# Graph attention block on one core: contexts before scores in every step

## Chip, cores and metric

One core of a Trainium2 chip. The metric is the device time of one execution in microseconds (us), here the median of three. One execution was also taken by the hardware profiler; the rows below are from it.

## What is computed

The input x is 128 graphs of 128 nodes with 384 features, adj is a 128x128 mask for each graph. All is float32.

```python
q = heads(x @ Wq + bq); k = heads(x @ Wk + bk); v = heads(x @ Wv + bv)   # 6 heads of 64
scores = einsum('bhqd,bhkd->bhqk', q, k) / sqrt(64)
probs = softmax(scores + where(adj, 0, -9e15)[:, None], axis=-1)
ctx = einsum('bhqk,bhkd->bhqd', probs, v)
y = x + (merge(ctx) @ Wf + bf)
out = (y - mean(y)) / sqrt(var(y) + 1e-5)      # over the 384 features
```

## The kernel before, in words

The work goes by **pairs** of graphs, 64 in all; a graph of a pair is called e=0 or e=1. Each engine has its own hand-written order of work, and semaphores alone join them. A **step** handles several stages of different pairs at once. In step p TensorE makes, in this order (`step`, L487):

- the scores of pair p (`scores`, L384; matmuls on L395): 6 heads for each graph, with 64 rows of the array each;
- the contexts of pair p-2 (`ctx_product`, L399; L413): 6 heads for each graph, with 64 columns of the array each;
- two of the three q/k products that this step has for a group of four graphs ahead (`qk_product`, L418), 9 matmuls of 512 columns each;
- the output products of pair p-2 (`out_product`, L429), 9 matmuls of 384 columns each;
- the third q/k product;
- the v products of pair p+2 (`early_v`, L444), again 9 of 384 columns each.

The q/k, output and v products are sums of three: high times high, low times high and high times low part (`split_product`, L375, matmuls on L379 to L381). So each operand has a high part, rounded by ScalarE, and a low part, which VectorE forms as the difference.

The banks of PSUM: `scores_ps` has two for each graph of the pair, `qk_ps` two, `cov_ps` one for each e. Three products share `cov_ps[e]` in turn: the contexts, the output product, and the v product. So before the contexts are made, `ctx_product` waits for `v_copied` of the previous step's v product, which ScalarE copies out (`copy_v`, L795); and before the v product is made, `early_v` waits for `y_added`, VectorE's addition of the output product and x (`add_residual`, L627; L638). `ctx_product` also waits for `pT_landed`: the probabilities are turned in blocks of 32x32 by VectorE, stored to DRAM and loaded again in transposed block order, all by DMAs of the SP queue (`store_blocks`, L288, and `load_blocks`, L295). `scores` waits for q and k (`qk_copied`) and until the scores of the pair before have been read (`max_found`).

VectorE in step p (`step`, L662): `mask_and_max` for both graphs (L606: adds the mask, scales, takes row maxima; L612 negates them), `split_ctx` (low parts of the contexts of pair p-2, L580), `turn_x` (transposes x of pair p+4, L588), `invert_sums` for e=0 (L625), `turn_blocks` for e=0 (L618), `invert_sums` for e=1, `split_x` for both (low parts of x^T of pair p+4, L595), `add_residual` for both (L638), then statistics of e=0, `turn_blocks` for e=1, and statistics of e=1.

ScalarE in step p (`step`, L810): `round_ctx` for both graphs (L781, high parts of the contexts), `exps` of e=0 (six on L790), a q/k copy (L807), `exps` of e=1, a q/k copy, `round_x` for both (high parts of x^T, L775), the third q/k copy, and the two copies of v (L798).

GpSimd in step p (`step`, L924): `make_mask_bias` for the two graphs of pair p+1 (L896; each waits until VectorE has read the mask of the same e, `max_found`), `add_bias` for both (L903), `normalise_probs` for both (L920, each waits for VectorE's inverted sums), `normalise_y` for pair p-2 (L909, L915).

`run_steps` (L82) writes the first steps out, runs a loop of four steps a turn, and writes the last out; step 61 is the last one of it. Pairs 62 and 63 are finished by `ending` (L527), which has its own order. Contexts begin in step 2, and v products on `cov_ps` end with step 59; x^T is also made ahead up to step 59.

Of the kernel before, what the change touches and what calls it, by code (L numbers as in the profile page):

```python
# [35 lines left out]
PAIRS = BATCH // 2  # L36
# [9 lines left out]
LAG = 2  # L46
# [22 lines left out]
def real(n, count):  # L69

    return not isinstance(n, int) or 0 <= n < count


def past(eng, sem, n, per=1):

    value = (n + 1) * per
    if isinstance(value, int) and value <= 0:
        return
    eng.wait_ge(sem, value)
# [14 lines left out]
def attention_block(nc, x, adj, wq, bq, wk, bk, wv, bv, wf, bf, out):  # L94
    ctx = ExitStack()
    with ctx:
# [81 lines left out]
        def ctx_bank(e, n):  # L178

            return qk_ps[e] if isinstance(n, int) and n >= 2 * (ENDING + 1) else cov_ps[e]  # L180
# [5 lines left out]
        def by_matmul(n):  # L186

            return isinstance(n, int) and n < BY_MATMUL
# [185 lines left out]
        def _(pe):  # L374
# [9 lines left out]
            def scores(i, c, e, n):  # L384
                par = c // 2 % 2
                if e == 0:
                    past(pe, qk_copied, 2 * i + c // 2, per=NJ)
                    if isinstance(n, int) and n == 0:
                        pe.wait_ge(xT_split, BY_MATMUL)
                        pe.wait_ge(bias_row_ready, 1)  # L390
                past(pe, max_found, n - 2)
                tok = tokens(2 * c + e)
                for h in range(HEADS):
                    rows = slice(h % 2 * HEAD, (h % 2 + 1) * HEAD)
                    last = nc.tensor.matmul(scores_ps[:, score_cols(e, h)], qT[rows, par, h // 2, tok],  # L395
                                            kT[rows, par, h // 2, tok], start=True, stop=True)
                last.then_inc(scores_done, 1)

            def ctx_product(i, c, p, e):  # L399
                n, at = 2 * (p - LAG) + e, 2 * (c - LAG) + e  # L400
                if isinstance(n, int) and n >= BY_VECTOR:
                    pe.wait_ge(pT_copied, 2 * (n - BY_VECTOR + 1))
                else:
                    past(pe, pT_landed[at % PT_RING], 2 * i + at // PT_RING, per=BLOCKS * DMA)
                if isinstance(p, int) and p - 1 + AHEAD >= ENDING:
                    past(pe, y_added, n - 2 if n < 2 * (ENDING + 1) else n - 4)
                    past(pe, v_copied, n)
                else:
                    past(pe, v_copied, 2 * (p - 1 + AHEAD) + e)
                dst = ctx_bank(e, n)  # L410
                for h in range(HEADS):
                    half = h % 2 * HEAD
                    last = nc.tensor.matmul(dst[half:half + HEAD, h // 2 * SEQ:(h // 2 + 1) * SEQ],  # L413
                                            v_sb[:, at % V_RING, h * HEAD:(h + 1) * HEAD],
                                            pT[:, at % PT_RING, :, h, :], start=True, stop=True)
                last.then_inc(ctx_done, 1)

            def qk_product(i, c, j):  # L418
                mat, m = QK_JOBS[j]
                g, par = 2 * i + (c + AHEAD) // 2, (c + AHEAD) // 2 % 2  # L420
                if isinstance(g, int) and g == 0:
                    pe.wait_ge(w_split[mat], m + 1)
                past(pe, xT_split, g * GROUP + GROUP - 1)
                past(pe, qk_copied, g * NJ + j - 2)
                split_product(qk_ps[j % 2][:, :], lambda k: (
                    w_hi[mat][:, k, m * P:(m + 1) * P], w_lo[mat][:, k, m * P:(m + 1) * P],
                    xT_hi[:, par, k, :], xT_lo[:, par, k, :]), qk_done)

            def out_product(c, p, e):  # L429
                n = 2 * (p - LAG) + e  # L430
                if isinstance(p, int) and p == LAG:
                    pe.wait_ge(w_split["f"], KC)
                pe.wait_ge(cT_split, n + 1)
                if isinstance(n, int) and n >= 2 * (ENDING + 1):
                    past(pe, y_added, n - 2)
                split_product(cov_ps[e][:, 0:HID], lambda k: (
                    cT_hi[:, e, k, :], cT_lo[:, e, k, :], w_hi["f"][:, k, :], w_lo["f"][:, k, :]), out_done)
# [6 lines left out]
            def early_v(c, p, e):  # L444
                n = 2 * (p + AHEAD) + e
                if isinstance(n, int) and n == 0:
                    pe.wait_ge(w_split["v"], KC)
                past(pe, xT_split, n)
                if real(p - LAG, PAIRS):
                    past(pe, y_added, 2 * (p - LAG) + e)  # L450
                else:
                    past(pe, v_copied, n - 2)
                v_product(cov_ps[e], 2 * (c + AHEAD) + e)
# [9 lines left out]
            def transpose_x(n):  # L463
                past(pe, x_loaded[n % X_RING], 0, per=DMA)
                past(pe, xT_split, n - 4)
                for k in range(KC):
                    last = nc.tensor.transpose(xT_bank(n)[:, k * SEQ:(k + 1) * SEQ],  # L467
                                               x_in[:, n % X_RING, k * P:(k + 1) * P], ident[:, :])
                last.then_inc(xT_done, 1)

            def warm_up(n):


                for _ in range(n):
                    nc.tensor.transpose(qk_ps[1][:, 0:P], ident[:, :], ident[:, :])  # L475

            def bias_product():

                pe.wait_ge(w_loaded["f"], DMA)
                pe.wait_ge(bv_widened, 1)  # L480
                pe.wait_ge(xT_split, GROUP + 1)
                for k in range(KC):
                    last = nc.tensor.matmul(xT_bank(0)[:, 0:HID], bv_wide[:, k, :], w_raw["f"][:, k, :],  # L483
                                            start=k == 0, stop=k == KC - 1)
                last.then_inc(bias_mm, 1)

            def step(i, c):  # L487
                p = TURN * i + c
                jobs = list(range(c % 2 * HALF, (c % 2 + 1) * HALF)) if real(p + AHEAD, PAIRS) else []
                if real(p, PAIRS):  # L490
                    for e in range(2):
                        scores(i, c, e, 2 * p + e)
                if real(p - LAG, PAIRS):
                    for e in range(2):
                        ctx_product(i, c, p, e)
                for j in jobs[:2]:
                    qk_product(i, c, j)
                if isinstance(p, int) and by_matmul(2 * (p + X_AHEAD)):
                    for e in range(2):
                        n = 2 * (p + X_AHEAD) + e  # L500
                        transpose_x(n)
                        if n in WARM_UPS:
                            warm_up(WARM_UPS[n])
                if isinstance(p, int) and p == -1:
                    bias_product()
                if real(p - LAG, PAIRS):
                    for e in range(2):
                        out_product(c, p, e)
                for j in jobs[2:]:
                    qk_product(i, c, j)  # L510
                if real(p + AHEAD, ENDING):
                    for e in range(2):
                        early_v(c, p, e)
# [50 lines left out]
            pe.wait_ge(ident_ready, 2)  # L564
            warm_up(WARM_UPS[-1])
            run_steps(pe, step, ENDING)
            ending()

# [414 lines left out]
```

## Time and profile before

| what | value |
|---|---|
| median of three runs | 1030.92 us (1030.38 to 1031.15) |
| the profiled execution | 1031.09 us |
| its span, first to last instruction | 1029.3 us |
| mean granted clock of TensorE | 0.999 |
| TensorE busy | 1017.5 us, 99% |
| weight loads | 906.5 us, 88% |
| VectorE busy | 732.1 us, 71% |
| GpSimd busy | 627.8 us, 61% |
| ScalarE busy | 596.4 us, 58% |

How to read it: an engine's busy time is the union of its instructions. TensorE's matmuls are pipelined, so that their durations overlap, and the distance from one start to the next is what counts. PE is TensorE, PEld its weight loads, DVE VectorE, ACT ScalarE, POOL GpSimd, and SPq the queue of the sync engine, which issues nearly all DMAs. One row of a timeline may stand for several instructions alike (x2, x24); its duration is then from the first's start to the last's end.

### The profile page before, as it was taken

How to read it: one execution, taken by the hardware profiler on the slowest of the kernel's cores; microseconds unless marked ns; L12 is line 12 of the kernel's file. 1: busy time of each engine (PE TensorE's matmuls, PEld its weight loads, DVE VectorE, ACT ScalarE, POOL GpSimd, SP SyncE). 2: the span in 40 equal slices, each digit the busy share in tenths (PEclk: the TensorE clock that was granted, in tenths of full speed). 3: DMA queues.
4: the chain of work that ended last, by engine and by line, in shares of the span. 5: the costliest groups of instructions: out<-in, count | busy, mean ns of one | idle time of the engine just before them, and what ended most of it. 6: DMA issues, size and time to landing. Idle time of an engine off the chain costs nothing.

```text
span 1029.3 us, 26790 instructions
## 1 busy us (share of the span) xinstructions
PE 1017.5 (99%) x7185; PEld 906.5 (88%) x7185; DVE 732.1 (71%) x2822; ACT 596.4 (58%) x2127; POOL 627.8 (61%) x649
## 2 busy tenths in 40 slices
PE   8999999999999999999999999999999999999996
PEld 7889889889888898898888898888988988988886
DVE  3576777777677777767776776777777677767674
ACT  4565655656646656556556466465565565564563
POOL 1355666656665756656666566656566666666675
PEclk9999999999999999999999999999999999999999
DMA  7286676676666666766766766766667667666431
GB/s 197 77 209 183 174 192 159 177 193 164 181 183 168 189 177 171 195 166 173 193 161 175 192 162 185 186 166 190 172 172 196 165 176 184 166 176 183 146 122 62
DMA packets 337690, 176.48 MB, mean 171 GB/s; under 512 B 222336, under 2 KB 321792, under 8 KB 337664
## 3 DMA queue, kind: packets, MB, share of 16 engines
q1 hardware_dynamic: 336864, 175.79, 62.7%
q10 hardware_dynamic: 800, 0.39, 0.1%
q8 instruction: 11, 0.18, 0.1%
q14 instruction: 15, 0.12, 0.0%
HBM read 102.18 MB, written 73.92 MB: 171 GB/s over the span
## 4 chain that ended last, share of the span: by engine, by line
PE 98%; DVE 1%; issue 0%; ACT 0%; POOL 0%; POOLq 0%; DVEq 0%
PE qk_ps L379 14%; PE qk_ps L381 13%; PE qk_ps L380 13%; PE cov_ps L379 13%; PE cov_ps L381 13%; PE cov_ps L380 13%; PE scores_ps L395 9%; PE cov_ps L413 9%; PE qk_ps L475 0%; PE scores_ps L523 0%; DVE s_mask L606 0%; DVE xT_lo L595 0%; PE scores_ps L467 0%; PE scores_ps L483 0%; PE qk_ps L413 0%
## 5 line engine op out<-in xcount | busy, mean ns | idle before, releaser
L790 ACT ACTIVATE probs<-s_mask,neg_max 128x128 f32<-128x128 f32 x756 | 292.6, 390 | 4.3 <-DVE neg_max L612 4.3
L606 DVE CUSTOM_DVE_ANT_0 s_mask<-scores_ps,mask_bias 128x128 f32<-128x128 f32 x768 | 172.5, 287 | 89.8 <-PE scores_ps L395 85.9
L920 POOL TENSOR_TENSOR probs<-probs,inv_sum 128x768 f32<-128x768 f32 x126 | 186.0, 1477 | 78.2 <-DVE inv_sum L625 78.2
L915 POOL TENSOR_SCALAR y_sb<-y_sb,mean_var,rstd 128x384 f32<-128x384 f32 x124 | 205.2, 1655 | 22.8 <-POOL rstd L909 22.8
L618 DVE STREAM_TRANSPOSE p_turned<-probs 128x768 f32<-128x768 f32 x124 | 121.3, 978 | 113.3 <-POOL probs L920 113.3
L909 POOL TENSOR_TENSOR rstd<-var_eps,minus_half 128x1 f32<-128x1 f32 x128 | 72.5, 566 | 180.3 <-DVE var_eps L653 180.3
L807 ACT ACTIVATE qT<-qk_ps,bq_col 128x512 f32<-128x512 f32 x96 | 65.6, 683 | 155.4 <-PE qk_ps L381 155.4
L790 ACT ACTIVATION_READ_ACCUMULATOR probs<-s_mask,neg_max 128x1 f32 x756 | 142.7, 189 | 0.0
L595 DVE TENSOR_TENSOR xT_lo<-xT,xT_hi 128x384 fp32r<-128x384 f32 x120 | 113.2, 981 | 32.8 <-ACT xT_hi L775 32.6
L781 ACT CAST cT_hi<-cov_ps 128x384 fp32r<-128x384 f32 x126 | 60.5, 480 | 125.8 <-PE cov_ps L413 123.0
L798 ACT COPY v_sb<-cov_ps 128x384 f32<-128x384 f32 x124 | 59.5, 480 | 122.0 <-PE cov_ps L381 122.0
L379 PE MATMUL cov_ps<-wf_hi,cT_hi 128*128 128x384 f32 x384 | 129.3, 337 | 0.0
L381 PE MATMUL cov_ps<-wf_hi,cT_lo 128*128 128x384 f32 x384 | 129.1, 336 | 0.0
L380 PE MATMUL cov_ps<-wf_lo,cT_hi 128*128 128x384 f32 x384 | 128.7, 335 | 0.0
L903 POOL TENSOR_TENSOR x_bias<-x_in,bias_row 128x384 f32<-128x384 f32 x128 | 127.6, 1019 | 0.0
L379 PE MATMUL cov_ps<-wv_hi,xT_hi 128*128 128x384 f32 x372 | 124.8, 336 | 0.9 <-DVE wv_lo L574 0.9
L381 PE MATMUL cov_ps<-wv_hi,xT_lo 128*128 128x384 f32 x372 | 124.9, 336 | 0.0
L380 PE MATMUL cov_ps<-wv_lo,xT_hi 128*128 128x384 f32 x372 | 124.7, 335 | 0.0
L379 PE MATMUL qk_ps<-xT_hi,wq_hi 128*128 128x512 f32 x288 | 116.0, 403 | 0.2 <-DVE xT_lo L595 0.2
L379 PE MATMUL qk_ps<-xT_hi,wk_hi 128*128 128x512 f32 x288 | 115.4, 401 | 0.0
L381 PE MATMUL qk_ps<-xT_hi,wq_lo 128*128 128x512 f32 x288 | 113.8, 395 | 0.0
L380 PE MATMUL qk_ps<-xT_lo,wq_hi 128*128 128x512 f32 x288 | 113.5, 394 | 0.0
(76 smaller groups left out, 2007.4 us busy)
## 6 DMA issues: line engine op xcount, KB each, us to landing
p_out<-p_turned SPq DMA_DIRECT2D x124, 384.0 KB, 2.6
pT<-p_out SPq DMA_DIRECT2D x496, 96.0 KB, 2.4
x_in<-in_x SPq DMA_DIRECT2D x128, 192.0 KB, 3.5
out<-y_sb SPq DMA_DIRECT2D x128, 192.0 KB, 2.4
x_blocks<-in_x SPq DMA_DIRECT2D x360, 64.0 KB, 2.3
adj_u<-in_adj SPq DMA_DIRECT2D x32, 64.0 KB, 3.3
probs<-in_L_gnn_Wv SPq DMA_DIRECT2D x1, 576.0 KB, 6.2
pT<-in_L_gnn_Wf SPq DMA_DIRECT2D x1, 576.0 KB, 6.8
```

Source lines behind the costliest of these rows:

```text
L379: nc.tensor.matmul(dst, s_hi, m_hi, start=k == 0, stop=False)
L380: nc.tensor.matmul(dst, s_hi, m_lo, start=False, stop=False)
L381: last = nc.tensor.matmul(dst, s_lo, m_hi, start=False, stop=k == n_chunks - 1)
L395: last = nc.tensor.matmul(scores_ps[:, score_cols(e, h)], qT[rows, par, h // 2, tok], kT[rows, par, h // 2, tok], start=True, stop=True)
L413: last = nc.tensor.matmul(dst[half:half + HEAD, h // 2 * SEQ:(h // 2 + 1) * SEQ], v_sb[:, at % V_RING, h * HEAD:(h + 1) * HEAD], pT[:, at ...
L595: nc.vector.tensor_tensor(xT_lo[:, par, :, tok], xT_source(n, e), xT_hi[:, par, :, tok].bitcast(F32), ALU.subtract).then_inc(xT_split, 1)
L606: last = nc.vector.tensor_tensor_reduce(out=s_mask[:, e, h, :], in0=scores_ps[:, score_cols(e, h)], in1=mask_bias[:, e, :], scale=SCALE, s ...
L618: nc.vector.transpose(p_turned[:, e, :, :, :].rearrange("p b h j -> p h b j"), probs[:, e, :, :].rearrange("p h (b k) -> p h b k", b=BLOCK ...
L790: last = nc.scalar.activation(p_sb[:, e, h, :], s_mask[:, e, h, :], ACT.Exp, bias=neg_max[:, e, h:h + 1], scale=1.0, accum_out=row_sum[:, ...
L903: nc.gpsimd.tensor_tensor(x_bias[:, slot, :], x_in[:, slot, :], bias_row[:, :], ALU.add).then_inc(x_biased, 1)
L915: nc.gpsimd.tensor_scalar(y_sb[:, y, :], y_sb[:, y, :], mean_var[:, e, 0:1], rstd[:, e, 0:1], ALU.subtract, ALU.mult).then_inc(y_ready, 1)
L920: nc.gpsimd.tensor_tensor(p_sb[:, e, :, :], p_sb[:, e, :, :], inv_sum[:, e, :].unsqueeze(2).broadcast_to([P, HEADS, SEQ]), ALU.mult).then_ ...
```

## The change

In TensorE's step the contexts of pair p-2 come first and the scores of pair p second. Nothing else is altered, neither the waits inside the two functions nor the order of any other engine, nor `ending`.

```diff
             def step(i, c):
                 p = TURN * i + c
                 jobs = list(range(c % 2 * HALF, (c % 2 + 1) * HALF)) if real(p + AHEAD, PAIRS) else []
+                if real(p - LAG, PAIRS):
+                    for e in range(2):
+                        ctx_product(i, c, p, e)
                 if real(p, PAIRS):
                     for e in range(2):
                         scores(i, c, e, 2 * p + e)
-                if real(p - LAG, PAIRS):
-                    for e in range(2):
-                        ctx_product(i, c, p, e)
                 for j in jobs[:2]:
                     qk_product(i, c, j)
```

## Rows read from the trace of the kernel before

**Rows 1.** The page, busy time of each engine (us, share of the span, instructions).

```profile
PE 1017.5 (99%) x7185; PEld 906.5 (88%) x7185; DVE 732.1 (71%) x2822; ACT 596.4 (58%) x2127; POOL 627.8 (61%) x649
```

**Rows 2.** Timeline of TensorE, step 30 (start us, us, engine, line, operation, tiles).

```profile
493.32 1.61 PE L395 MATMUL scores_ps<-kT,qT 64*128 64x128 f32 x24
494.86 1.53 PE L413 MATMUL cov_ps<-pT,v_sb 128*64 128x128 f32 x24
496.32 0.50 PE L379 MATMUL qk_ps<-xT_hi,wq_hi 128*128 128x512 f32 x1
...
500.53 0.33 PE L379 MATMUL cov_ps<-wf_hi,cT_hi 128*128 128x384 f32 x1
...
508.98 1.61 PE L395 MATMUL scores_ps<-kT,qT 64*128 64x128 f32 x24
```

**Rows 3.** Timeline of VectorE, step 30.

```profile
497.47 0.09 DVE L606 DVE_READ_ACCUMULATOR2_ANT row_max<- 128x1 f32 x1
...
497.67 1.01 DVE L580 TENSOR_TENSOR cT_lo<-cov_ps,cT_hi 128x384 fp32r<-128x384 f32 x2
...
501.52 0.98 DVE L618 STREAM_TRANSPOSE p_turned<-probs 128x768 f32<-128x768 f32 x1 [1.83 <-POOL probs L920]
...
503.13 1.88 DVE L595 TENSOR_TENSOR xT_lo<-xT,xT_hi 128x384 fp32r<-128x384 f32 x2 [0.55 <-ACT xT_hi L775]
504.93 1.01 DVE L638 TENSOR_TENSOR y_sb<-cov_ps,x_bias 128x384 f32<-128x384 f32 x2
```

**Rows 4.** Timeline of GpSimd, step 30.

```profile
497.70 0.30 POOL L896 TENSOR_SCALAR mask_bias<-adj_u 128x128 f32<-128x128 uint8 x1 [1.30 <-issue]
497.97 2.00 POOL L903 TENSOR_TENSOR x_bias<-x_in,bias_row 128x384 f32<-128x384 f32 x2
499.91 1.48 POOL L920 TENSOR_TENSOR probs<-probs,inv_sum 128x768 f32<-128x768 f32 x1
502.65 1.47 POOL L920 TENSOR_TENSOR probs<-probs,inv_sum 128x768 f32<-128x768 f32 x1 [1.26 <-DVE inv_sum L625]
```

**Rows 5.** Timeline of ScalarE and of TensorE's weight loads, step 30.

```profile
496.43 0.48 ACT L781 CAST cT_hi<-cov_ps 128x384 fp32r<-128x384 f32 x1 [0.17 <-PE cov_ps L413]
496.81 0.40 ACT L790 ACTIVATE probs<-s_mask,neg_max 128x128 f32<-128x128 f32 x1
...
505.59 0.19 PEld L379 LDWEIGHTS cov_ps<-wv_hi,xT_hi 128*128 128x128 f32 x1
...
509.08 0.48 ACT L798 COPY v_sb<-cov_ps 128x384 f32<-128x384 f32 x1 [1.08 <-PE cov_ps L381]
```

**Rows 6.** Timeline of step 1, which has no contexts.

```profile
43.20 1.61 PE L395 MATMUL scores_ps<-kT,qT 64*128 64x128 f32 x24
...
45.92 0.40 ACT L790 ACTIVATE probs<-s_mask,neg_max 128x128 f32<-128x128 f32 x1 [2.14 <-DVE neg_max L612]
...
52.24 2.30 DVE L595 TENSOR_TENSOR xT_lo<-xT,xT_hi 128x384 fp32r<-128x384 f32 x2
...
52.28 1.85 POOL L920 TENSOR_TENSOR probs<-probs,inv_sum 128x768 f32<-128x768 f32 x1 [1.16 <-DVE inv_sum L625]
...
54.47 0.96 DVE L618 STREAM_TRANSPOSE p_turned<-probs 128x768 f32<-128x768 f32 x1
```

**Rows 7.** Timeline of the end of step 7 and the start of step 8.

```profile
144.04 0.55 DVE L595 TENSOR_TENSOR xT_lo<-xT,xT_hi 128x384 fp32r<-128x384 f32 x1
...
144.51 1.01 DVE L638 TENSOR_TENSOR y_sb<-cov_ps,x_bias 128x384 f32<-128x384 f32 x2
...
148.50 0.38 PE L395 MATMUL scores_ps<-kT,qT 64*128 64x128 f32 x2
```

**Rows 8.** Busy time of each engine in two stretches, granted clock, DMA.

```profile
15.00:20.00 5.00, 4.11 (x23) 3.65 (x22) 4.21 (x8) 2.40 (x5) 2.61 (x5) 1.00 0.80 143
1020.00:1029.00 9.00, 2.09 (x13) 1.77 (x11) 5.45 (x16) 0.00 (x0) 1.98 (x3) 0.88 0.24 88
```

## The prediction

> **What bounds the kernel now.** I first read the page's busy times, to see which engine sets the time: TensorE is busy 99% of the span, the next engine 71% [rows 1]. Next TensorE's timeline over one step, to see the order and whether there are holes: the scores of pair 30 start at 493.32, the contexts of pair 28 at 494.86, the q/k products at 496.32, the output products at 500.53, the next scores at 508.98 [rows 2]. A step is 15.66 us without a hole. The scores block holds 1.54 us, the contexts block 1.46.
>
> That only says that TensorE is never late now. What counts is how late its inputs may come, so I then read VectorE, GpSimd and ScalarE in the same step. Write S for the start of the scores. The last maximum is read at 497.47 (S+4.15). GpSimd's second mask waits for it (497.70), then come the two x+bias (497.97, 2.00 us for both) and the first normalisation of the probabilities (499.91, 1.48) with no gap [rows 3, 4]. VectorE waits for that, turns the blocks (501.52) and inverts the second sums; this releases GpSimd's second normalisation (502.65 to 504.12). The low parts of x^T start at 503.13 and the two take 1.88, where one without GpSimd beside it takes 0.55 [rows 7]: the first is not finished until GpSimd is. The residual additions start at 504.93. Two take 1.01 overlapping by 0.08 (503.13+1.88 against 504.93), so one takes 0.545 and the first ends at 505.47, **S+12.15** [rows 3, 4]. The v product that follows overwrites the bank which this addition reads, and its first weight load is at 505.59, 0.12 later [rows 5]. TensorE starts no weight load more than one matmul ahead, so a hole would open if this one came much later. So a chain of 12.15 us, which starts with the scores and runs through the other engines, is only just in time for the v product; I put its slack at 0 to 0.1 us.
>
> **The change, part by part.** It adds and removes nothing: per step 24 context and 24 score matmul records trade places; no DMA and no queue but TensorE's is touched. Call C the start of the step.
>
> 1. *TensorE's own time*: the same three changes of shape (v to first block, first to second, second to q/k). In today's order the blocks hold 1.54 and 1.46, 3.00 together [rows 2]; I take 3.00 again, 0. Bounds: plus or minus 0.05 a step.
>
> 2. *The wait of the second context for its bank.* The contexts write the banks that ScalarE copies v out of. The copy of the second v runs 509.08 to 509.56, 0.58 after the step's start [rows 5]; today 1.54 us of scores cover it. With the 0.12 us from a finish to the weight load behind it, the second context could load at C+0.70, and its matmuls follow when half the block, 0.73, has passed; now the load can't run ahead of them. Between 0 and 0.15 us; I take 0.08, the middle.
>
> 3. *The scores and all that hangs on them start later*: at C+1.46+0.08 = C+1.54. That is the cost that matters, since the chain of 12.15 us hangs on S, and the v product's place in TensorE's order hangs on C. Unchanged, the addition would end at C+13.69 where it now ends at S+12.15.
>
> 4. *What gets shorter in the chain.* ScalarE's first exponentials now start at 496.81 (S+3.49), behind the high part of the second context (496.43, 0.48) [rows 5]. In pair 1, which has no contexts yet, they start at 45.92, S+2.72, as soon as the maxima are there [rows 6]. After the change the contexts come first, so ScalarE follows pair 1, and the high parts of x^T, which follow the exponentials on it, come 0.77 earlier. But that alone doesn't shorten the chain, since GpSimd's part (mask, x+bias, normalisation) hangs on the maxima and not on ScalarE. Pair 1 shows what then happens: VectorE starts the first low part at 52.24, S+9.04, just before GpSimd starts its normalisation at 52.28. The first low part is through at once, the normalisation takes 1.85 instead of 1.47, the second low part waits for it, and the pair ends at 54.54, S+11.34 [rows 4, 6]. An addition of 0.545 that begins at 54.47 (where pair 1 has its next work) ends at 55.015, **S+11.81**. Pair 1 has no low parts of contexts on VectorE; I add 0.03 for them and take **S+11.84**.
>
> The Trainium skill ("SBUF — State Buffer", section "Who interferes with whom") says of this that a VectorE instruction with two SBUF inputs and a GpSimd instruction that reads SBUF exclude each other, and that the first to issue keeps the ports for its whole length. The 1.85 us of rows 6 agree. By the rule alone the order of 52.24 and 52.28 decides the case, as in the first rival below.
>
> 5. *From the addition to the next step.* Where the addition already came a little late, it began at 144.51 (first one over at 145.055) and the next step began at 148.50: 3.45 us [rows 7]. Late release costs nothing beyond this; VectorE, ScalarE and GpSimd have their later work behind TensorE's v products as now.
>
> Sum of a step: 1.54 + 11.84 + 3.45 = 16.83 us, against 15.66: **+1.17 us**, all of it TensorE standing before the v product. It hits the steps that have contexts, low parts of x^T and a v product: pairs 2 to 59, 58 steps, 67.9 us. In pairs 60 and 61 no v product waits; the end sees the scores of pair 61 later by between 0 and 1.5 us, of which I take half, 0.7. Together 68.6. The profiled execution took 1031.09 (span 1029.30), 0.17 over the median of 1030.92: 1030.92 + 68.6 = **1099.5 us**.
>
> *What stays covered.* The output products need the low parts of the contexts: the first pair of these starts at 497.67, and one takes 0.54, so S+4.89; that becomes C+6.43 and TensorE wants them at C+7.21 [rows 2, 3]. The probabilities' way through DRAM: VectorE has the first half of pair 30 turned at 502.50, the second some 6 us later, and the contexts read them two steps on, at 494.86+31.3 = 526.2; 17 us for a store and a load, of which 3.1 go (scores 1.54 later, contexts 1.54 earlier). If these covers were gone, each us would count 58 times.
>
> **The rivals.**
> - *GpSimd's normalisation comes first.* The 0.04 us in pair 1 is a knife's edge. If GpSimd wins, both low parts wait for it: today's order, with the normalisation at pair 1's S+9.08 plus the same 0.03 in place of today's S+9.33 [rows 4, 6], so the addition ends 0.22 before S+12.15, at S+11.93: +1.26 a step, 73.1+0.7, **1104.7 us**.
> - *Nothing in the chain gets shorter*: S+12.15 stays: 1.54+12.15+3.45 = 17.14, +1.48 a step, 85.8+0.7, **1117.4 us**. For it: the steady steps all show S+12.15. Against it: pair 1, and that GpSimd's last y ends earlier against S once the step is longer.
> - *Not slower*: both low parts pass ahead of the normalisation. Then they run from S+9.04 to about S+10.1, the addition ends at S+10.6 = C+12.1, and the v product is in time. It decides at C+12.2: below this, no stall. With the copy of v also early enough (item 2 at 0) the time is **1031 us**, with 0.08 a step 1035.6. Against it: in pair 1 the second low part stood directly behind the first on VectorE and yet lost to GpSimd [rows 6].
> - *The clock*: the granted clock is 1.00 in a stretch with TensorE busy 4.11 of 5 us and 0.88 in the last 9 us, where it is busy 2.09 [rows 8]. A hole of 1.2 us in 16.8 is nearer to the first. If one step in ten ran at 1.2 instead of 2.4 GHz, it would take some 15 us longer: 1099.5+5.8x15, **1186 us**. The Trainium skill ("TensorE: Matmul & The Clock Gate", Part 1) has the clock halve after idleness; both rows agree with that, and neither shows it for holes this short.
> - The change does what it says: no other place sets the order of the two blocks on TensorE, and the steps of the loop all pass through it.
>
> **How the numbers follow.** Forecast 0.45, GpSimd first 0.25, nothing shorter 0.12, not slower 0.05, clock 0.03; 0.10 for a stall that is shorter or longer through something I don't see. The likeliest gives 1099.5. Downwards item 2 at 0 takes 4.6 off, item 1 2.9, the end 0.7, and the unseen shorter chains reach somewhat further: 1086. Upwards "nothing shorter" sets 1118. Not slower splits into 0.03 within 0.2% (some 2 us, about what a measurement of this kernel can tell from no change) and 0.01 below; its rest is slower.
>
> **What would show it.** Right: a step of 16.8 us; a hole of about 1.2 us on TensorE before the first weight load of the v product, released by VectorE's residual addition; exponentials at S+2.7; the first low part of x^T short and the normalisation beside it 1.85. If both low parts are in one long pair and the normalisation 1.47, it is the first rival. Wrong: the hole stands elsewhere (before the second context, or before the output products), or the step stays near 15.7.

## The result, and the profile after

The changed kernel took a median of 1104.73 us (1104.40 to 1105.13) against 1030.67 for the kernel before on the same chip: a ratio of 1.0717, 95% interval 1.0700 to 1.0734. It is 74.1 us slower, or 1.28 us for each of the 58 steps that the forecast counts. The forecast was 1099.5 us (1086 to 1118), slower with 0.96.

The page of the profile after: span, busy times, TensorE's granted clock in 40 slices, and the chain that ended last.

```profile
span 1102.6 us, 26790 instructions
...
PE 1036.0 (94%) x7185; PEld 901.9 (82%) x7185; DVE 749.0 (68%) x2822; ACT 602.3 (55%) x2127; POOL 644.2 (58%) x649
...
PEclk9999999999999999999999999999999999999999
...
PE 40%; issue 26%; POOL 18%; DVE 13%; DVEq 1%; ACT 1%; POOLq 0%; ACTq 0%
```

The instructions are as many as before. TensorE's share falls from 99% [rows 1] to 94%, and no other engine rises. The chain has moved off TensorE: GpSimd and VectorE now hold a third of it.

TensorE's waits after, by what ended them (us in total, times, longest):

```profile
PE cov_ps L379 <- DVE y_sb L638: 55.0, 58, 1.0
```

One wait, 58 times: the first matmul of the v product for VectorE's residual addition. These 55.0 us are counted from modelled ends of matmuls, and the hole costs more than that. By starts, in the step below, the v product begins 1.36 us after the last q/k matmul (557.57 to 558.93), and in step 30 before 0.23:

```profile
505.53 0.40 PE L381 MATMUL qk_ps<-xT_hi,wq_lo 128*128 128x512 f32 x1
505.76 0.34 PE L379 MATMUL cov_ps<-wv_hi,xT_hi 128*128 128x384 f32 x1
```

Its second matmul follows 0.25 later instead of 0.18. That makes 1.20 us a step, some 70 us; the rest of the 1.28 is in the contexts' block, as shown further down.

Step 31 after, TensorE (start us, us; C is 545.29 and S is 546.83):

```profile
545.29 1.61 PE L413 MATMUL cov_ps<-pT,v_sb 128*64 128x128 f32 x24
546.83 1.61 PE L395 MATMUL scores_ps<-kT,qT 64*128 64x128 f32 x24
...
552.58 0.33 PE L379 MATMUL cov_ps<-wf_hi,cT_hi 128*128 128x384 f32 x1
...
557.57 0.40 PE L381 MATMUL qk_ps<-xT_hi,wq_lo 128*128 128x512 f32 x1
558.93 0.41 PE L379 MATMUL cov_ps<-wv_hi,xT_hi 128*128 128x384 f32 x1 [0.96 <-DVE y_sb L638]
...
562.22 1.53 PE L413 MATMUL cov_ps<-pT,v_sb 128*64 128x128 f32 x24
```

The same step on VectorE, on ScalarE, and on GpSimd:

```profile
550.98 0.08 DVE L606 DVE_READ_ACCUMULATOR2_ANT row_max<- 128x1 f32 x1
...
555.93 0.15 DVE L625 RECIPROCAL inv_sum<-row_sum 128x6 f32<-128x6 f32 x1
556.01 2.30 DVE L595 TENSOR_TENSOR xT_lo<-xT,xT_hi 128x384 fp32r<-128x384 f32 x2
558.24 1.01 DVE L638 TENSOR_TENSOR y_sb<-cov_ps,x_bias 128x384 f32<-128x384 f32 x2
```

```profile
545.40 0.48 ACT L798 COPY v_sb<-cov_ps 128x384 f32<-128x384 f32 x1 [1.08 <-PE cov_ps L381]
...
549.69 0.40 ACT L790 ACTIVATE probs<-s_mask,neg_max 128x128 f32<-128x128 f32 x1 [2.28 <-DVE neg_max L612]
```

```profile
551.21 0.30 POOL L896 TENSOR_SCALAR mask_bias<-adj_u 128x128 f32<-128x128 uint8 x1 [1.38 <-issue]
...
556.15 1.74 POOL L920 TENSOR_TENSOR probs<-probs,inv_sum 128x768 f32<-128x768 f32 x1 [1.26 <-DVE inv_sum L625]
```

Read against [rows 2 to 5]: C to S is 1.54 in this step. The last maximum is read at S+4.15, as before. The exponentials start at S+2.86 instead of S+3.49 and now wait for the maxima instead of the contexts' high parts. GpSimd's second mask is at S+4.38, where it was. The low parts of x^T start at S+9.18, before GpSimd's second normalisation at S+9.32. That normalisation takes 1.74 instead of 1.47, the pair of low parts 2.30 instead of 1.88, and it is over at S+11.48, where it was over at S+11.69. The first addition ends at 558.24+0.545 = 558.785, which is S+11.95, and the next step begins 3.44 later. 1.54 + 11.95 + 3.44 = 16.93 us, where a step took 15.66.

The four steps of a loop turn are not alike. Steps 32 and 33:

```profile
562.22 1.53 PE L413 MATMUL cov_ps<-pT,v_sb 128*64 128x128 f32 x24
563.68 1.61 PE L395 MATMUL scores_ps<-kT,qT 64*128 64x128 f32 x24
...
579.07 1.68 PE L413 MATMUL cov_ps<-pT,v_sb 128*64 128x128 f32 x24
580.68 1.61 PE L395 MATMUL scores_ps<-kT,qT 64*128 64x128 f32 x24
```

C to S is 1.46 in the first step of a turn, 1.61 in the second and third and 1.54 in the fourth, the same in every turn; the mean of the 58 steps is 1.55. In the old order the contexts' block holds 1.46 in each step. S to the first addition is 11.94 to 11.97 in nearly all steps of the loop. The whole step has a mean of 16.95 us against 15.67.

### The profile page after: what moved, and what is told of

The parts are those of the page before. It is cut to its first block, busy times and chain, and to the rows that moved or that the text cites. A ratio compares the mean times of both kernels' runs of the same rounds, so it can differ in the third digit from the quotient of the medians.

```text
span 1102.6 us, 26790 instructions
## 1 busy us (share of the span) xinstructions
PE 1036.0 (94%) x7185; PEld 901.9 (82%) x7185; DVE 749.0 (68%) x2822; ACT 602.3 (55%) x2127; POOL 644.2 (58%) x649
## 4 chain that ended last, share of the span: by engine, by line
PE 40%; issue 26%; POOL 18%; DVE 13%; DVEq 1%; ACT 1%; POOLq 0%; ACTq 0%
POOL x_bias L903 9%; PE cov_ps L413 9%; DVE s_mask L606 8%; PE cov_ps L379 8%; POOL probs L920 8%; PE cov_ps L381 6%; PE cov_ps L380 6%; PE scores_ps L395 5%; DVE y_sb L638 3%; PE qk_ps L379 1%; PE qk_ps L380 1%; PE qk_ps L381 1%; DVEq L79 1%; DVE xT_lo L595 1%; DVE inv_sum L625 1%
## 5 line engine op out<-in xcount | busy, mean ns | idle before, releaser
L920 POOL TENSOR_TENSOR probs<-probs,inv_sum 128x768 f32<-128x768 f32 x126 | 201.5, 1600 | 78.1 <-DVE inv_sum L625 78.1
L379 PE MATMUL cov_ps<-wv_hi,xT_hi 128*128 128x384 f32 x372 | 128.9, 347 | 55.9 <-DVE y_sb L638 55.0
L896 POOL TENSOR_SCALAR mask_bias<-adj_u 128x128 f32<-128x128 uint8 x128 | 38.1, 298 | 188.4 <-DVE row_max L606 103.3
L595 DVE TENSOR_TENSOR xT_lo<-xT,xT_hi 128x384 fp32r<-128x384 f32 x120 | 138.2, 1192 | 0.2
L379 PEld LDWEIGHTS cov_ps<-wv_hi,xT_hi 128*128 128x128 f32 x372 | 69.7, 187 | 80.2 <-DVE xT_lo L595 78.7
```

The source lines that it names most:

```text
L379: nc.tensor.matmul(dst, s_hi, m_hi, start=k == 0, stop=False)
L595: nc.vector.tensor_tensor(xT_lo[:, par, :, tok], xT_source(n, e), xT_hi[:, par, :, tok].bitcast(F32), ALU.subtract).then_inc(xT_split, 1)
L920: nc.gpsimd.tensor_tensor(p_sb[:, e, :, :], p_sb[:, e, :, :], inv_sum[:, e, :].unsqueeze(2).broadcast_to([P, HEADS, SEQ]), ALU.mult).then_ ...
```

## The experiments

Each time below stands beside one of the kernel before, whose median was 1030.8 to 1031.2 us in these sets. The first four experiments ask whether the chain from the scores to the addition carries the cost.

**1. Additions ahead of the low parts, contexts first.** On VectorE, in the changed kernel:

```diff
                     invert_sums(1, 2 * p + 1)
+                if real(p - LAG, PAIRS):
+                    for e in range(2):
+                        add_residual(i, c, e, 2 * (p - LAG) + e)
                 if real(p + X_AHEAD, PAIRS):
                     for e in range(2):
                         split_x(c, e, 2 * (p + X_AHEAD) + e)
...
                 if real(p - LAG, PAIRS):
-                    for e in range(2):
-                        add_residual(i, c, e, 2 * (p - LAG) + e)
                     find_stats(c, 0, 2 * (p - LAG))
```

> The changed order, and on VectorE the two residual additions moved ahead of the two low parts of x^T. Theory: the change costs time only because the additions stand at the end of a chain that starts with the scores, and the v product waits for them. The additions then end by about S+10.3 (S: start of the scores), which is C+11.8 (C: start of the step), ahead of the v product's place at C+12.2; the hole of 1 us goes, the step is 15.67 us plus 0 to 0.1 for the second context's wait for the copy of v, and the time is 1031 to 1037 us. Rival: the order itself costs TensorE time (changes of shape, the contexts' wait): then nothing comes back, about 1104 us.

Measured: 1037.06 us (1036.42 to 1037.13), ratio 1.0055 (1.0038 to 1.0071). Of the 74.1 us, 68.2 are gone. VectorE and TensorE in a step of it (S is 513.69):

```profile
522.78 0.15 DVE L625 RECIPROCAL inv_sum<-row_sum 128x6 f32<-128x6 f32 x1
522.85 0.98 DVE L638 TENSOR_TENSOR y_sb<-cov_ps,x_bias 128x384 f32<-128x384 f32 x2
523.75 1.62 DVE L595 TENSOR_TENSOR xT_lo<-xT,xT_hi 128x384 fp32r<-128x384 f32 x2
```

```profile
512.15 1.61 PE L413 MATMUL cov_ps<-pT,v_sb 128*64 128x128 f32 x24
513.69 1.61 PE L395 MATMUL scores_ps<-kT,qT 64*128 64x128 f32 x24
...
522.41 0.33 PE L381 MATMUL cov_ps<-wf_hi,cT_lo 128*128 128x384 f32 x1
...
524.66 0.33 PE L379 MATMUL cov_ps<-wv_hi,xT_hi 128*128 128x384 f32 x1
...
527.90 1.53 PE L413 MATMUL cov_ps<-pT,v_sb 128*64 128x128 f32 x24
```

The additions are over by 523.83, the v product starts at 524.66 with no wait before it, and the contexts still come first. So of the cost of the new order 0.10 us a step stays, and the rest came with the place of the additions on VectorE. The output products, which the additions read, start their last matmul at 522.41, half a microsecond before the additions here; in the changed kernel it starts 2.7 us before them (555.55 against 558.24).

**2. The same additions with the old order**, as the control.

> The old order with the additions ahead of the low parts on VectorE, as the control of the last. Theory: TensorE has no hole to fill, so within 0.2% of 1030.7 us. If the additions' slack was costing something already, up to 0.1 us a step comes back: 1025 us at the lowest.

Measured: 1031.39 us, ratio 1.0002 (0.9992 to 1.0012). No change: TensorE had no hole that earlier additions could close.

**3. The second inversion behind the low parts, contexts first.** This keeps the additions in place and takes GpSimd's normalisation out of the way of the low parts:

```diff
                     invert_sums(0, 2 * p)
                     turn_blocks(i, c, 0, 2 * p)
-                    invert_sums(1, 2 * p + 1)
                 if real(p + X_AHEAD, PAIRS):
                     for e in range(2):
                         split_x(c, e, 2 * (p + X_AHEAD) + e)
...
+                if real(p, PAIRS):
+                    invert_sums(1, 2 * p + 1)
```

> The changed order, and on VectorE the second inversion of sums, which releases GpSimd's second normalisation, moved behind the two low parts of x^T. Theory (the second low part waits because GpSimd's normalisation takes the shared access between the two): both low parts now run in 1.03 us from S+9.1, the first addition ends at S+10.7 instead of S+11.95, that is C+12.25, the step falls from 16.95 to 15.75 us, the time to 1034 to 1042 us. Rival (the second low part is late for its own reasons, such as the high part from ScalarE at S+9.56 or VectorE's rate): the pair still ends near S+11.4 and the time stays near 1100 us.

Measured: 1037.33 us, ratio 1.0060 (1.0044 to 1.0077). A step of it (S is 513.30), VectorE and GpSimd:

```profile
522.48 1.03 DVE L595 TENSOR_TENSOR xT_lo<-xT,xT_hi 128x384 fp32r<-128x384 f32 x2
523.42 0.18 DVE L625 RECIPROCAL inv_sum<-row_sum 128x6 f32<-128x6 f32 x1
523.52 0.98 DVE L638 TENSOR_TENSOR y_sb<-cov_ps,x_bias 128x384 f32<-128x384 f32 x2
```

```profile
523.69 1.47 POOL L921 TENSOR_TENSOR probs<-probs,inv_sum 128x768 f32<-128x768 f32 x1 [2.31 <-DVE inv_sum L625]
```

The two low parts start at S+9.18 as before, take 1.03 us instead of 2.30, and the normalisation 1.47 instead of 1.74. Of the second low part's 1.8 us in the changed kernel, 1.27 were the wait for GpSimd. That is the "not slower" rival's mechanism brought about by hand. The Trainium skill ("SBUF — State Buffer", section "Who interferes with whom") says that a VectorE instruction with two SBUF inputs contends with a GpSimd instruction that reads SBUF, and that the order of issue decides which of them waits. The traces agree in both directions (1.74 against 1.47, 2.30 against 1.03).

**4. One context first.** The order is context 0, both scores, context 1:

```diff
                 if real(p - LAG, PAIRS):
-                    for e in range(2):
-                        ctx_product(i, c, p, e)
+                    ctx_product(i, c, p, 0)
                 if real(p, PAIRS):
                     for e in range(2):
                         scores(i, c, e, 2 * p + e)
+                if real(p - LAG, PAIRS):
+                    ctx_product(i, c, p, 1)
```

> Half the change: the context of graph 0, both scores, then the context of graph 1. The scores move by half as much, to C+0.78, and no context waits for the copy of v, but ScalarE's exponentials stand behind the second context again, and TensorE changes shape once more (0.1 us). Theory: C to S 0.78, S to the end of the first addition 12.15, then 3.46, a step of 16.39 us, 58 x 0.72 = 42 us more than before: 1073 us, and if GpSimd's or ScalarE's earlier end counts, S+11.95 and 1061 us. Rival (any context ahead of the scores costs the whole): 1104 us.

Measured: 1062.97 us, ratio 1.0307 (1.0290 to 1.0324). TensorE, ScalarE and VectorE in a step of it:

```profile
524.95 0.88 PE L413 MATMUL cov_ps<-pT,v_sb 128*64 128x128 f32 x12
525.75 1.61 PE L395 MATMUL scores_ps<-kT,qT 64*128 64x128 f32 x24
527.29 0.88 PE L413 MATMUL cov_ps<-pT,v_sb 128*64 128x128 f32 x12
541.15 0.88 PE L413 MATMUL cov_ps<-pT,v_sb 128*64 128x128 f32 x12
```

```profile
528.21 0.48 ACT L782 CAST cT_hi<-cov_ps 128x384 fp32r<-128x384 f32 x1 [1.86 <-PE cov_ps L413]
528.61 0.40 ACT L791 ACTIVATE probs<-s_mask,neg_max 128x128 f32<-128x128 f32 x1
```

```profile
537.16 1.01 DVE L639 TENSOR_TENSOR y_sb<-cov_ps,x_bias 128x384 f32<-128x384 f32 x2
```

C to S is 0.80, the first addition ends at 537.705 = S+11.95, the next step comes 3.45 later: 16.20. The chain is as long as in the full change, the scores move by half, and the cost is 32 of 74 us. (The view of TensorE's waits lists only 0.2 us on the additions in the whole run here, though the v product starts 0.53 us after the last q/k matmul, where 0.23 is usual: again the modelled ends.) It is less than half because the first 0.27 us of the shift cost nothing: 0.20 by which the chain got shorter and 0.07 of slack (experiment 7). 0.80 - 0.27 = 0.53 us a step here, and 1.54 - 0.27 = 1.27 in the full change. The expectation's main value, 1073, was wrong: it kept S+12.15 because ScalarE's exponentials would stand behind the second context. They do stand behind its high part, but that is done in time: they start at 528.61, which is S+2.86, as in the full change. The second value, 1061, was near.

The next three ask why the chain was 0.11 us longer than forecast, and how much slack the old kernel had.

**5. The loop written out**, contexts first, so that each wait is against a constant:

```diff
-    with eng.Fori(1, turns) as i:
-        for c in range(TURN):
-            step(i, c)
+    for p in range(TURN, turns * TURN):
+        step(p // TURN, p % TURN)
```

> The changed kernel with the loop of four steps a turn written out, so that every wait is against a constant. Theory: the forecast's chain was read from step 1, ahead of the loop, and came out 0.14 us too short because in the loop, where waits are computed from a register, the chain's hand-overs take longer. Written out, the first addition ends at S+11.81 in all steps, a step is 16.81 instead of 16.95 us, and the time falls by 56 x 0.14 = 7.8 to about 1097 us. Rival (the longer chain comes from what runs beside it in the steady state, not from the loop): S+11.95 stays, 1104.7 us.

Measured: 1097.06 us, ratio 1.0642 (1.0622 to 1.0661), 7.7 us less than the changed kernel. Its step 31, VectorE and GpSimd (S is 544.12):

```profile
548.12 0.08 DVE L605 DVE_READ_ACCUMULATOR2_ANT row_max<- 128x1 f32 x1
...
553.16 2.30 DVE L594 TENSOR_TENSOR xT_lo<-xT,xT_hi 128x384 fp32r<-128x384 f32 x2
555.38 1.01 DVE L637 TENSOR_TENSOR y_sb<-cov_ps,x_bias 128x384 f32<-128x384 f32 x2
```

```profile
553.21 1.84 POOL L919 TENSOR_TENSOR probs<-probs,inv_sum 128x768 f32<-128x768 f32 x1 [1.16 <-DVE inv_sum L624]
```

The first addition ends at 555.925 = S+11.81, which is to the hundredth what the forecast read from step 1, and the normalisation's 1.84 us is within 0.01 of step 1's. So the missing 0.14 us belongs to the loop. C to S is 1.54 here in all steps too, so the pattern of four goes with the loop as well.

The traces also show where in the chain it arises. The last maximum is read at S+4.00 here and at S+4.15 in the changed kernel, and what follows is later by the same: GpSimd's second mask 4.38 against 4.23, the first low part 9.18 against 9.04. Of the 0.15, 0.06 lie between the scores and VectorE's first mask (1.18 against 1.12), and 0.09 between the maxima of e=0 and the first mask of e=1, where VectorE passes its waits (from the negation to the next mask 0.31 against 0.22). The run writes the waits out and takes the loop's turns away together, so it doesn't show which of the two it is.

**6. The loop written out, old order.**

> The old kernel with its loop written out, the control of the last. Theory: the chain gets shorter here too (the first addition ends at S+11.93 instead of S+12.15), but TensorE already waits for nothing, so 1030.7 us within 0.2%. Rival (loop turns cost TensorE time themselves): up to 14 turns of 0.1 to 0.5 us less.

Measured: 1031.52 us, ratio 1.0007 (0.9997 to 1.0017). The chain got shorter here too, to S+11.93 from S+12.15, but that brings nothing where TensorE is the bound.

**7. The old order with a longer chain.** On VectorE, four reciprocals of the second sums into a spare tile ahead of the real one:

```diff
             def invert_sums(e, n):
                 past(dve, exp_done, n)
                 past(dve, probs_ready, n - 2)
+                for k in range(4 * e):
+                    nc.vector.reciprocal(spare[:, k, :], row_sum[:, e, :])
                 nc.vector.reciprocal(inv_sum[:, e, :], row_sum[:, e, :]).then_inc(sum_inverted, 1)
```

> The old order with four more reciprocals of the second sums into a spare tile, ahead of the one that releases GpSimd, so that the chain gets longer by d while the order on TensorE stays. Theory: the old kernel's slack is 0 to 0.1 us, so of d nearly all appears as a hole before the v product: with four reciprocals of 0.08 to 0.15 us, d is 0.3 to 0.6, the step gets 0.2 to 0.6 longer, and the time is 1043 to 1066 us. Rival (there is more slack than that, and the changed order hurts through something else): the time stays within 0.3% of 1030.7 us.

Measured: 1042.45 us, ratio 1.0114 (1.0096 to 1.0132). VectorE, then TensorE (S is 514.27):

```profile
523.38 0.35 DVE L627 RECIPROCAL spare<-row_sum 128x6 f32<-128x6 f32 x4
...
526.15 1.01 DVE L641 TENSOR_TENSOR y_sb<-cov_ps,x_bias 128x384 f32<-128x384 f32 x2
```

```profile
514.27 1.61 PE L396 MATMUL scores_ps<-kT,qT 64*128 64x128 f32 x24
...
530.14 1.39 PE L396 MATMUL scores_ps<-kT,qT 64*128 64x128 f32 x20
```

The first addition ends at S+12.42 instead of S+12.15, 0.27 later, and the step is 15.87 us instead of 15.67, the old kernel's mean: 0.20 of the 0.27 arrive. The old kernel's slack is about 0.07 us. The time is just under the range expected, because a reciprocal adds 0.07 us and not 0.08 to 0.15.

The last two ask what the 6 us are that stay with the additions first.

**8. A later copy of v**, with contexts and additions first. ScalarE copies the second v once more, into a spare tile, ahead of the real copy:

```diff
             def copy_v(bank, slot, n):
                 past(act, v_done, n)
                 past(act, ctx_done, n - V_RING)
+                if bank is cov_ps[1]:
+                    nc.scalar.copy(spare[:, slot // 2, :], bank[:, 0:HID])
                 nc.scalar.copy(v_sb[:, slot, :], bank[:, 0:HID]).then_inc(v_copied, 1)
```

> Contexts first and additions first (1037.1 us), and ScalarE copies the second v of each pair once more, into a spare tile, ahead of the real copy, which so ends about 0.4 us later. Theory: what is left of the changed order's cost (0.1 us a step) is the second context's wait for this copy, so the step gets longer by the whole 0.4 us: 58 x 0.4 = 23, 1056 to 1062 us. Rival (the 0.1 us is a dearer change of shape on TensorE, and the copy has slack): under 1040 us.

Measured: 1059.65 us, ratio 1.0280 (1.0263 to 1.0297). TensorE, then ScalarE:

```profile
522.45 0.88 PE L414 MATMUL cov_ps<-pT,v_sb 128*64 128x128 f32 x12
523.56 0.88 PE L414 MATMUL cov_ps<-pT,v_sb 128*64 128x128 f32 x12 [0.24 <-ACT v_sb L802]
```

```profile
522.55 0.48 ACT L801 COPY spare<-cov_ps 128x384 f32<-128x384 f32 x1 [1.08 <-PE cov_ps L382]
522.93 0.48 ACT L802 COPY v_sb<-cov_ps 128x384 f32<-128x384 f32 x1
```

The copy comes 0.38 later, and 22.6 us come on top of experiment 1: 0.39 a step. The second context starts 1.11 after the first, 0.15 after the copy is over. So the second context hangs on the copy with no slack to speak of. In experiments 1 and 3 the contexts' block holds 1.55 us in the mean, against 1.46 in the old order: of the 0.10 us a step left there, 0.09 is this wait.

**9. One context first, additions first**, the edits of experiments 4 and 1 together.

> Context 0, scores, context 1, with the additions first on VectorE. No context waits for the copy of v; TensorE changes shape once more, which took 0.15 us a step in the run with one context first. Theory: nothing else is left, a step of 15.82 us, 58 x 0.15 = 8.7 us more than before: 1040 us. Rival (something else in the early scores or contexts costs time too): over 1043 us.

Measured: 1040.94 us, ratio 1.0097 (1.0080 to 1.0114), 10.0 us over the kernel before, or 0.17 a step: the 0.15 of one more change of shape, and 0.02 whose cause is open. No version beat the kernel before.

## Why the prediction was right

*What bounds the kernel.* That TensorE's 99% hid a chain only just in time held: experiment 7 measures a slack of about 0.07 us, where 0 to 0.1 was given.

*Item 1, TensorE's own time:* 0 was forecast, and that held. The scores' block takes 1.54 us in both orders, and the contexts' block 1.46 in one step of four in the new order too.

*Item 2, the second context's wait:* 0.08 was forecast. The contexts' block is 0.09 longer in the mean (1.55 against 1.46), and experiment 8 shows that it is the copy. That the wait differs between the steps of a turn was not foreseen.

*Item 3, the chain hangs on the scores:* C to S was forecast as 1.54 and is 1.55 in the mean. Experiments 1 and 4 show it from two sides, with the chain cut and with half the shift.

*Item 4, what gets shorter:* the mechanism was right in each part. ScalarE's exponentials wait for the maxima (at S+2.86, where 2.7 was forecast), the first low part gets in ahead of GpSimd's normalisation, and the second waits for it (the normalisation takes 1.74, where 1.85 was forecast). The size is the term that was off: the forecast put the end of the first addition at S+11.84, and it is S+11.95. It was read from step 1, which stands ahead of the loop, and experiment 5 gives S+11.81 in its step 31 and 11.82 in the mean once there is no loop. The 0.14 us that the loop adds on this chain are missing from the term (the 0.03 for the contexts was not needed). The trace before could have shown it: in [rows 3] the last maximum is at S+4.15, in step 1 at S+4.00, and in steps 2 and 3, which have contexts but stand ahead of the loop, the first addition ends at S+11.93 and S+11.94, not at S+12.15. The forecast's "nothing shorter" rival counted against itself that GpSimd's last y would end earlier against S. It did (S+1.28 after, S+2.81 before), but the second mask stayed at S+4.38, so this y is not on the chain.

*Item 5:* 3.45 forecast, 3.44 measured.

*Steps and end:* with S+11.95 the sum is 1.54 + 11.95 + 3.45 = 16.94, 1.28 more than 15.66, times 58 is 74.2. The measured difference is 74.1. The 0.7 us for the end was not needed: from the end of the 58th step to the last instruction it is 65.8 us in both profiles (963.54 to 1029.3 and 1036.82 to 1102.6).

*The rivals.* "GpSimd's normalisation comes first" gave 1104.7, the measured value, but by luck, since its mechanism didn't happen: the normalisation started at S+9.32 and not at the 9.11 that the rival took, and the first low part was ahead of it, so that it took 1.74 and not 1.47. The two errors nearly cancel in the end of the addition (S+11.93 for S+11.95), and its 0.7 us for the end made up the rest. "Nothing shorter" fell with S+11.95. "Not slower" did not happen, though experiment 3 shows that its mechanism was one place in VectorE's order away. The clock stayed: 9 in all 40 slices.

## What to carry to other kernels

When the bounding engine is full, look for the last input that is only just in time, and write down which earlier block on the same engine starts its chain: moving that block back costs most of that time in every step, here 1.28 of 1.54 us. The cheap remedy is often on another engine: two additions placed behind work that they don't need made the order on TensorE matter, and placing them first took back 68 of 74 us. Read chain lengths from steps inside the loop, and from all steps of a turn: the same instructions ahead of it ran 0.14 us faster, and the contexts' block took 1.46 to 1.61 us by the step's place in the turn.

## What the runs showed of the hardware

- A loop on the engines costs time on the chain between them: S to the first addition is 11.95 us in the loop and 11.81 with it written out. Writing it out brought 7.7 us where the chain was the bound and nothing (ratio 1.0007) where TensorE was. The traces put all of it ahead of VectorE's last maximum (S+4.15 against S+4.00).
- The same wait can end at different times in the steps of one loop turn: the contexts' block takes 1.46, 1.61, 1.61 and 1.54 us in turn, and 1.54 in every step with the loop written out. The cause is open.
- Two VectorE instructions of two SBUF inputs, back to back, do not keep GpSimd out: in the steps of the changed kernel's loop GpSimd's normalisation got in between them, and the pair took 2.30 us against 1.03 alone (experiment 3).
- One more change between score and context matmuls takes about 0.15 us a step: in experiment 4 the q/k products start 3.15 us after C, against 3.00 in [rows 2].
